# Values of twelve full steps of a pair in three fp16 products, with halves made by ScalarE and GpSimd

## The reference

```python
q = ln @ Wq
kv_input = jnp.concatenate((xn, ln), axis=1)
kv = kv_input @ Wkv
k, v = jnp.split(kv, 2, axis=-1)
q, k, v = (heads(q) * scale, heads(k), heads(v))
sim = jnp.einsum('bhid,bhjd->bhij', q, k)
sim = jnp.where(mask_full[:, None, None, :], sim, max_neg)
attn = jax.nn.softmax(sim.astype(jnp.float32), axis=-1).astype(sim.dtype)
out = jnp.einsum('bhij,bhjd->bhid', attn, v)
out = out.transpose(0, 2, 1, 3).reshape(b, m, INNER)
out = out @ Wout
```

## Time and profile before

| | us |
|---|---|
| median of 3 runs | 904.13 |
| lowest and highest of them | 903.83, 904.18 |
| the profiled execution, its own time | 903.74 |
| its span, first to last instruction | 901.8 |
| PE busy | 830.0 |
| DVE busy | 598.5 |
| ACT busy | 451.4 |
| POOL busy | 186.7 |

### The profile page before, as it was taken

How to read it: one execution, slowest core, us unless ns; L and a number is a source line. 1 busy time by engine, 2 the same in 40 slices (tenths; PEclk the granted TensorE clock), 3 DMA queues, 4 the chain that set the end, 5 groups by cost and what they waited for, 6 DMA issues and landing times.

```text
span 901.8 us, 20739 instructions
## 1 busy us (share of the span) xinstructions
PE 830.0 (92%) x6742; PEld 444.4 (49%) x6743; DVE 598.5 (66%) x1517; ACT 451.4 (50%) x756; POOL 186.7 (21%) x353
## 2 busy tenths in 40 slices
PE   5699999999999999999999999999999999999653
PEld 4344545545454555545454545455454545455412
DVE  5786666666757566766666575767666576647587
ACT  5365455545455545545455554455464646443142
POOL 3011021212222221211122222212022222212101
PEclk9799999999999999999999999999999999999665
DMA  6113221111212111101212111111112111110001
GB/s 202 36 41 103 79 56 46 47 39 51 57 40 55 50 54 54 55 20 52 57 44 57 47 53 52 55 52 44 32 51 57 40 55 50 46 35 16 4 1 47
DMA packets 98347, 45.82 MB, mean 51 GB/s; under 512 B 72100, under 2 KB 90376, under 8 KB 98184
## 3 DMA queue, kind: packets, MB, share of 16 engines
q1 hardware_dynamic: 98256, 45.34, 18.3%
q10 hardware_dynamic: 56, 0.05, 0.0%
HBM read 25.69 MB, written 3.26 MB: 32 GB/s over the span
## 4 chain that ended last, share of the span: by engine, by line
PE 71%; DVE 16%; issue 7%; ACT 3%; DMA 1%; DVEq 1%; POOL 1%; ACTq 0%; SPq 0%; POOLq 0%
PE bank L1296 20%; PE bank L1350 7%; PE bank L1269 6%; PE bank L1224 5%; PE bank L1273 4%; PE bank L1271 4%; DVE mx L1690 4%; PE bank L1241 4%; PE bank L1367 3%; PE bank L1411 3%; DVE xf_all L1719 3%; PE bank L1386 2%; PE bank L1396 2%; PE bank L1240 2%; ACT arena L967 1%
## 5 line engine op out<-in xcount | busy, mean ns | idle before, releaser
L982 ACT ACTIVATE p<-bank,maskbias 128x512 f32<-128x512 f32 x224 | 154.3, 689 | 232.6 <-PE bank L1273 231.1
L1296 PE MATMUL bank<-p,xv 128*128 128x512 f32 (+1 forms) x512 | 238.0, 616 | 0.3 <-POOL arena L836 0.3
L1690 DVE TENSOR_REDUCE mx<-bank 128x1 f32<-128x512 f32 x256 | 165.5, 682 | 53.1 <-PE bank L1241 52.7
L1686 DVE TENSOR_TENSOR qkl_l<-bank,qkl_h 128x512 f16<-128x512 f32 x64 | 41.1, 685 | 76.7 <-ACT qkl_h L970 76.7
L1296 PEld LDWEIGHTS bank<-p,xv 128*128 128x128 f32 (+1 forms) x512 | 74.9, 188 | 31.5 <-issue 23.8
L1269 PE MATMUL bank<-qkc_h,xtT_h 128*128 128x512 f16 (+1 forms) x256 | 86.9, 389 | 0.0
L1241 PE MATMUL bank<-xtT_h,qkc_h 128*128 128x448 f16 x256 | 86.7, 358 | 0.0
L1271 PE MATMUL bank<-qkc_l,xtT_h 128*128 128x512 f16 (+1 forms) x256 | 85.0, 379 | 0.0
L1273 PE MATMUL bank<-qkc_h,xtT_l 128*128 128x512 f16 (+1 forms) x256 | 85.0, 379 | 0.0
L1240 PEld LDWEIGHTS bank<-ltT,qkl_h 128*128 128x128 f16 x256 | 24.9, 98 | 95.4 <-DVE mx L1690 53.8
L1350 PE MATMUL bank<-arena,wvF 128*64 128x128 f32 x1024 | 69.3, 278 | 0.0
(11 more groups left out here) (261 smaller groups left out, 1462.1 us busy)
## 6 DMA issues: line engine op xcount, KB each, us to landing
arena<-den_dram SPq DMA_DIRECT2D x62, 128.0 KB, 3.1
qkc_h<-arena SPq DMA_DIRECT2D x30, 256.0 KB, 2.4
qkc_l<-arena SPq DMA_DIRECT2D x30, 256.0 KB, 2.5
raw<-in_ctx SPq DMA_DIRECT2D x32, 192.0 KB, 2.4
raw<-in_ctx SPq DMA_DIRECT2D x64, 32.0 KB, 2.2
lt<-lt_dram SPq DMA_DIRECT2D x60, 31.8 KB, 2.1
arena<-in_L_xattn_Wkv SPq DMA_DIRECT2D x1, 1024.0 KB, 6.8
ltT_dram<-x_all SPq DMA_DIRECT2D x4, 256.0 KB, 3.2
```

What stands on the lines that cost most here:

```text
L982: a.activation(p32[0:r, slot, :], sbank[t % SRING][0:r, :], ACT.Exp, bias=bias).then_inc(s_probs_ready, 1)
L1296: op = mm(bk[:, :], rows_of[at, :], p32[at, slot, :], start=tile < 2, stop=tile in (0, plan.TILES - 1))
L1690: v.tensor_reduce(mx[:, hq_tile, part:part + 1], bk[:, 0:width], AX.X, ALU.max).then_inc(s_jobs_taken, 1)
```

## The change

The probabilities of the full steps (t >= `SPLIT` = 2) and the rows of the three full tiles are kept as two fp16 halves each, in the same bytes that held one fp32 value.

- **ACT** (`probs`) runs the exponential of a full step twice: into the upper fp16 half (`p_halves[..., 0, :]`) and in fp32 into `p_all`, which has two places. The first of them waits until POOL is done with the step two full steps earlier (`s_p_lo`). Only the second sets `probs_ready`.
- **POOL** (`low_probs`, new) subtracts the upper half from the fp32 value and writes the lower half, 128x512, once per full step, as the last of its work in that step. These instructions are called low2 to low7 below. In `prep` the copy of the rows becomes a cast to fp16 (128x381), a subtraction of the same size that waits for the cast, and a copy of the 127 columns of the short tile.
- **PE** (`values`) waits for the lower half and makes three fp16 products (upper x upper, lower rows x upper, upper rows x lower) in place of one fp32 product. Short steps stay in fp32.
- One weight buffer and the `ones` columns of `xv` are moved or set in another place.

```diff
--- before.py
+++ after.py
...
@@ -133,6 +135,10 @@
 
         tile, half = self.steps[t]
         return P if half is None or tile > 1 else (M, self.TAIL)[tile]
+
+    def split_index(self, b, t):
+
+        return b * self.SPLITS + t - self.SPLIT
 
     def chunk(self, tile):
 
...
@@ -384,7 +393,7 @@
         mask32 = p32[0:B, :, :].rearrange("p a b -> p (a b)")[:, 0:N + M]
         mask8 = qkl_l[:, :, :].rearrange("p k c -> p (k c)").bitcast(U8)[0:B, 0:N]
 
-        aw = words(11008, 4, D)
+        aw = words(10240, 4, D)
         fw = words(8192, 768).rearrange("p (g c n) -> p g c n", g=2, c=3)
         fwd = words(8960, FF)
         diag = words(9312, D)
@@ -401,6 +410,9 @@
         qkn_h = words(8192, 1024).bitcast(F16).rearrange("p (k c) -> p k c", k=2)
         qkn_l = words(9216, 1024).bitcast(F16).rearrange("p (k c) -> p k c", k=2)
         kexp = words(10240, 2, AH // 2, M)
+        p_all = words(11264, 2, HALF)
+        p_halves = p32[:, :, :].rearrange("p a b -> p (a b)").bitcast(F16).rearrange("p (a h b) -> p a h b", a=RING, h=2)
+        xv_halves = xv[:, :, :, :].rearrange("p a c d -> p (a c d)").bitcast(F16).rearrange("p (a c h d) -> p a c h d", a=2, c=WHOLE.CH, h=2)
         tsc = words(12288, AH, M)
         pT = words(13312, 8, P)
 
...
@@ -806,9 +817,20 @@
                         if happened((n - 1) * plan.STEPS):
                             pool.wait_ge(s_values_done, (n - 1) * plan.STEPS)
                         g.tensor_copy(maskbias[:, par, 0:CH], mask_bias[plan][:, bass.ds(n, 1), :].rearrange("p o c -> p (o c)")).then_inc(s_maskbias_ready, 1)
-                    op = g.tensor_copy(xv[:, par, c0:c1, 0:127], raw[:, par, c0:c1, 0:127])
+                    split = min(c1, plan.FULL)
+                    g.tensor_copy(xv_halves[:, par, c0:split, 0, 0:127], raw[:, par, c0:split, 0:127]).then_inc(s_xv_hi, 1)
+                    pool.wait_ge(s_xv_hi, n * len(at["XV"]) + list(at["XV"]).index(t) + 1)
+                    op = g.tensor_tensor(xv_halves[:, par, c0:split, 1, 0:127], raw[:, par, c0:split, 0:127], xv_halves[:, par, c0:split, 0, 0:127], ALU.subtract)
                     if c1 == CH:
+                        op = g.tensor_copy(xv[:, par, plan.FULL, 0:127], raw[:, par, plan.FULL, 0:127])
                         op.then_inc(s_xv_ready, 1)
+
+            def low_probs(plan, i, k, t):
+
+                if t >= plan.SPLIT:
+                    b, slot = i * 2 + k, slot_of(plan, k, t)
+                    pool.wait_ge(s_probs_ready, b * plan.STEPS + t + 1)
+                    g.tensor_tensor(p_halves[:, slot, 1, :], p_all[:, (t - plan.SPLIT) % 2, :], p_halves[:, slot, 0, :], ALU.subtract).then_inc(s_p_lo, 1)
 
             def tail(plan, p, s):
 
@@ -845,6 +867,9 @@
                     g.tensor_tensor(srs[:, 2:3], sve[:, 2:3], nhalf[:, 0:1], ALU.pow).then_inc(s_rstd_b, 1)
 
             def attention(plan):
+                g.memset(xv_halves[:, :, 0:plan.FULL, 0, 127:128], 1.0)
+                g.memset(xv_halves[:, :, 0:plan.FULL, 1, 127:128], 0.0)
+                g.memset(xv[:, :, plan.FULL, 127:128], 1.0).then_inc(s_xv_ones, 1)
                 pool.wait_ge(s_mask_made, 1)
                 for t in range(plan.STEPS):
                     ahead(plan, 0, 0, t)
...
@@ -979,6 +1005,13 @@
                 if t == plan.LAT:
                     act.wait_ge(s_maskbias_ready, b + 1)
                 bias = zrow[0:r, :] if tile == 0 else maskbias[0:r, k, plan.chunk(tile):plan.chunk(tile) + 1]
+                if t >= plan.SPLIT:
+                    f = plan.split_index(b, t)
+                    if happened(f - 1):
+                        act.wait_ge(s_p_lo, f - 1)
+                    a.activation(p_halves[:, slot, 0, :], sbank[t % SRING][:, :], ACT.Exp, bias=bias)
+                    a.activation(p_all[:, (t - plan.SPLIT) % 2, :], sbank[t % SRING][:, :], ACT.Exp, bias=bias).then_inc(s_probs_ready, 1)
+                    return
                 a.activation(p32[0:r, slot, :], sbank[t % SRING][0:r, :], ACT.Exp, bias=bias).then_inc(s_probs_ready, 1)
 
             def copy_context_part(plan, b, pair, k, h):
@@ -1280,7 +1313,10 @@
             def values(plan, b, k, t):
                 tile, half = plan.steps[t]
                 slot = slot_of(plan, k, t)
-                pe.wait_ge(s_probs_ready, b * plan.STEPS + t + 1)
+                if t >= plan.SPLIT:
+                    pe.wait_ge(s_p_lo, plan.split_index(b, t) + 1)
+                else:
+                    pe.wait_ge(s_probs_ready, b * plan.STEPS + t + 1)
                 halves = (0, 1) if half is None else (half,)
                 if tile == 0 and happened(2 * b - 1 + max(halves)):
                     pe.wait_ge(s_uc_copied, 2 * b - 1 + max(halves))
@@ -1292,6 +1328,10 @@
                 parts = [(ubank[hf], slice(r * hf, r * hf + r) if half is None else slice(0, r)) for hf in halves]
                 c = plan.chunk(tile)
                 rows_of = lt[:, k, :] if tile == 0 else xv[:, k, c, :]
+                if t >= plan.SPLIT:
+                    for rows, probs in ((0, 0), (1, 0), (0, 1)):
+                        op = mm(ubank[half][:, :], xv_halves[:, k, c, rows, :], p_halves[:, slot, probs, :], start=False, stop=tile == plan.TILES - 1 and probs == 1)
+                    parts = []
                 for bk, at in parts:
                     op = mm(bk[:, :], rows_of[at, :], p32[at, slot, :], start=tile < 2, stop=tile in (0, plan.TILES - 1))
                 op.then_inc(s_values_done, 1)
```

7 lines of the change are left out of this document (6 added, 1 removed).

## The result

| | before | after |
|---|---|---|
| median, us (runs) | 903.98 (4) | 938.38 (4) |
| lowest and highest | 901.55, 904.18 | 935.69, 940.26 |
| profiled execution, span | 901.8 | 938.5 |
| a pair in the loop | 50.05 | 51.65 |

The changed kernel takes 1.0383 times as long, with a 95% interval of 1.0365 to 1.0400: 3.8% slower, some 34 us. The forecast was 929 us with a range of 908 to 950, and 0.85 for slower. The direction and the range held; the forecast itself is 9 us too low.

The account below looks back on a forecast made before the run. PE, busy 92% of the span, was taken to bound the kernel. Loop +24 us, first pair -1 and last pair +1.5 made about +25 on the profiled 903.7, or 929 us, range 908 to 950 (about 80%).

Parts of the forecast that it names:

- What bounds, and what PE saves: Full values steps: PE bounds the kernel; three fp16 products save 0.21 us a step, 2.5 us a pair.
- rival in which PE keeps most of the 2.5 us: Loop: subtractions at 0.5 us or less, without detour, let POOL keep up; 866 to 895 us, 12% chance.
- ACT costs nothing: Full steps: 192 more exponentials, 8.3 us a pair, cost nothing on PE's path except a later start of POOL's part.
- The price of the subtraction: POOL, each full step: 128x512 subtraction takes 1.27 us, with 1.07 and 1.74 kept for the range.
- low4 late at s14: Second half of a pair: POOL's subtraction stands behind `rstd`, so its values start 0.85 us late.
- DVE's detour: Second half of a pair: DVE's four row scalings wait for POOL's subtractions; rows ready 1.15 us later.
- `kexp` and the way round: Before s0': `kexp` ends at 433.3, PE goes on 2.3 us later; v6, v7, v2, v3 recover some, leaving +1.0 at s6.
- low6 behind the 128x1024 subtraction: First half, s8: POOL's queue and DVE's held scaling delay the values by 2.1 us, leaving +1.7 us a pair.
- The loop's sum: Some 14 of 16 pairs at +1.7 us each, 24 us in all.
- The first pair: First pair of the program: saves about 1 us.
- Last pair and end: Last pair: v2 to v5 save 0.85 us, v7 comes some 2.5 us later, +1.5 in sum; nothing changes after.
- the cheaper case: Loop: subtractions at 1.07 us, or no DVE waiting for POOL, give 908 to 918 us; 17% chance.

## Why the prediction was right, point by point

- **What bounds, and what PE saves.** Right in the size: PE's busy time fell by 2.2 us a pair, with 2.5 worked out. But without any subtraction PE keeps only 1.37 us of it, 1.1 us less than the 2.5 worked out, where the prediction named the 0.42 of v2 and v3 as swallowed by DVE. So its rival in which PE keeps most of the 2.5 us (866 us at the lower end) was out of reach: the run without a subtraction took 881.
- **ACT costs nothing.** Right as far as PE's steps go, shown by the run with one exponential. The rows' halves cost nothing either: they take 1.7 us of POOL (2.1 estimated), and without the subtraction of the probabilities s2 and s10 are as long as before.
- **The price of the subtraction.** 1.168 us instead of 1.27, so 0.1 too high per instruction, halfway to the lower bound of 1.07. By the prediction's own scheme this takes 0.3 to 0.4 us off a pair.
- **low4 late at s14.** Right in place; 0.51 us of wait where 0.85 was worked out: the subtraction is cheaper, and PE itself comes later.
- **DVE's detour.** Right in kind: the scalings went from 1.09 to 1.94, +0.85 where 1.15 was worked out. The step that failed is what was left out of it. The prediction looked for the port only at the scalings, and `rcol` at s11 paid it as well: +0.94 us inside DVE's unbroken stretch, which moved `ve` and everything behind it on POOL. Counted from the scores of s12, the values of s0' come 2.9 us later than before, where 2.3 was worked out.
- **`kexp` and the way round.** The wait before s0' is 1.54 us ("1.5 us or more"), PE no longer waits for `xtT_l` behind v6 (from v6 to s1' 0.65 us less, as worked out), and the steps of v7, v2 and v3 are 0.31, 0.11 and 0.21 us shorter, together the 0.63 that was worked out.
- **low6 behind the 128x1024 subtraction.** Right in place, with one part that did not happen. Counted from the scores of s9 (476.79 us, before 410.21), the values of the next s8 come 1.9 us later than before; 2.1 was worked out. PE's idle time ahead of them is only 0.62 us where about 1.5 was named: more of the delay was already in PE's work by then, for s6 starts 1.6 us late, counted from s12, where 1.0 was worked out. And the scaling of the rows in this half, which was to wait for low5, is not held. It starts just as low5 ends, and takes its 1.09 us:

```profile
518.51 1.09 DVE L1696 TENSOR_SCALAR raw<-raw,mv,rstd 128x128 f32<-128x128 f32 x4
```

  So the forecast had too little delay up to s6 (no `rcol`) and too much behind it (a hold that did not happen, a dearer subtraction, a longer wait). That these cancel to 51.65 against a forecast of 51.8 is luck.
- **The loop's sum.** 14 times 1.7 is 24; measured from the third to the fifteenth pair, 13 of them, 23.6, of which 3.2 are the two iterations with a lower granted clock, a term that the prediction did not have.
- **The first pair: wrong, and the largest miss.** "The first pair saves about 1 us" became +8.3. The prediction took its PE saving and looked at neither queue. There POOL has `srs` (L790) for DVE to normalise with, and the preparation puts three groups of four SBUF instructions (`xf_all`) on DVE, beside the scalings of the rows, which take 2.16 us instead of 1.09 and 1.10. DVE's line for one such group, changed kernel and then before:

```profile
64.67 1.94 DVE L1568 TENSOR_SCALAR xf_all<-xf_all,smv,srs 128x127 f32<-128x127 f32 x4 [0.53 <-POOL srs L790]
```

```profile
63.48 1.11 DVE L1528 TENSOR_SCALAR xf_all<-xf_all,smv,srs 128x127 f32<-128x127 f32 x4 [0.53 <-POOL srs L779]
```

  PE waits behind it, 1.73 us instead of 0.73, and behind a later group 2.85 instead of 1.66; twice it waits 0.76 us for a lower half. In the pair's second half its granted clock is 0.83, where it was 1.00 before. The first pair before, to be held against its line in the table above:

```profile
37.57:83.25 45.68, 42.77 (x287) 20.59 (x288) 35.08 (x110) 26.19 (x44) 7.32 (x13) 0.95 0.21 59
```

  Of the 8.3 us, 4.65 are idle time of PE (7.56 against 2.91) and 3.64 are busy time (46.41 against 42.77), although PE has less to do. The second part is the lower clock (0.85 against 0.95 in the two lines). With 64 columns subtracted in this pair both are mostly gone (4.17 us idle, 42.57 busy). Which part of the wait would have been there with the clock of before was not taken apart.
- **Last pair and end: mis-sized.** +6.5 instead of +1.5. The named term is there: v7 waits 2.56 us (2.5 worked out).

```profile
858.43 0.82 PE L1333 MATMUL bank<-p,xv 128*128 128x512 f16 x3 [2.56 <-POOL p L833]
```

  What was missing is the port again. The quantisation of the feed-forward weights on DVE, short instructions from SBUF to SBUF, is held three times for the length of a subtraction (at 845.01, 846.84 and 849.12, 1.06 to 1.08 us each); of one kind there stand side by side:

```profile
844.30 0.23 DVE L1616 TENSOR_SCALAR arena<-arena 128x128 f32<-128x128 f32 x1
...
845.01 1.08 DVE L1616 TENSOR_SCALAR arena<-arena 96x128 f32<-96x128 f32 x1
```

  and PE, which transposes them, waits 2.13 us before L1203 where it waited 0.24. The remainder, some 1.7 us from v7 to the end, is not explained: the mean granted clock there is 0.66, before 0.65, and no run was made on it.

Between the forecast's sum (24 - 1 + 1.5 = 24.5) and the difference of the two spans (36.7) are 12.2 us: the first pair makes 9.3 of them and the end 5.0; setup and the second pair give 1.6 back, and the loop 0.4, the longer iterations included. The median of after lies 1.9 us below the profiled execution.

That the total stayed in the range says little for the terms outside the loop: the first pair and the end are together 14.3 us beyond the forecast.

The rivals: the cheaper case was half true in its premise (1.168) and false in its result. The rival in which POOL keeps up was tried with half the columns: with 0.674 us a subtraction the kernel is 0.8% faster than before. POOL is busy for 26.88 us a pair, where 29 was worked out. Three products read as one row of 0.82 us, and a single product of the scores as 0.38, so the starts are 0.22 us apart, as in the earlier trace rows. (The 131 ns that the Trainium skill, "TensorE: Matmul & The Clock Gate", Back-to-back issue gap, gives for a steady stream is not seen in this kernel, and nothing came of that rival.)

## What to carry to other kernels

When a helper engine gets work that others wait for, its busy share says little: at 47% busy, POOL cost the pair 3 us, and the same work, with the order of POOL and of PE's wait changed, an estimated 0.3. So write out what stands in front of each urgent result on that engine, and put the work without slack first. And where GpSimd and VectorE both work from SBUF, look for every VectorE instruction of a kind that is held (below) and can meet a GpSimd one, and count it at its price plus what is left of the other, in the first and last pair as much as in the loop.
